# Softmax shifts and q laid in their rows by DMA instead of PE transposes and ScalarE copies, in an exact masked-attention layer

## The reference

```python
qkv = layer_norm(x, g1, be1) @ w_qkv            # (n, 3, 8, 16)
scores = einsum('nhd,mhd->hnm', q, k) * 16**-0.5
scores = where(adj != 0, scores, -inf)
out = einsum('hnm,mhd->nhd', softmax(scores, -1), v)
x = x + out @ w_proj + b_proj
x = x + gelu(layer_norm(x, g2, be2) @ w1 + b1) @ w2 + b2
```

## Time and profile before

| | |
|---|---|
| median of 3 runs | 1792.54 us (1791.68 to 1794.93) |
| profiled execution | 1792.59 us, span 1790.8 us |
| mean granted TensorE clock | 0.97 |
| first weighing of tile 4's step 3 to that of tile 5 | 204.25 us |

### The profile page before, as it was taken

How to read it: one execution, slowest core, us unless ns; L and a number is a source line. 1 busy time by engine, 2 the same in 40 slices (tenths; PEclk the granted TensorE clock), 3 DMA queues, 4 the chain that set the end, 5 groups by cost and what they waited for, 6 DMA issues and landing times.

```text
span 1790.8 us, 46610 instructions
## 1 busy us (share of the span) xinstructions
PE 1640.1 (92%) x17058; PEld 516.3 (29%) x17058; DVE 1411.1 (79%) x4471; ACT 1322.5 (74%) x1475; POOL 1198.3 (67%) x1129
## 2 busy tenths in 40 slices
PE   6989999999999999999999999999999999999975
PEld 3422222323223232323223232323223232223213
DVE  6888879877898779887898779988799778987501
ACT  4547877787877877787777878777777878778771
POOL 4945587578856777468856788558865788557441
PEclk9869999999999999999999999999999999999995
DMA  7710036202450035301360035301362024400000
GB/s 213 173 42 2 19 107 119 55 1 66 128 110 2 13 101 119 73 1 55 113 121 17 2 97 129 78 2 42 109 106 48 2 77 125 78 2 2 8 7 6
DMA packets 168711, 115.08 MB, mean 64 GB/s; under 512 B 139297, under 2 KB 149026, under 8 KB 168482
## 3 DMA queue, kind: packets, MB, share of 16 engines
q1 hardware_dynamic: 157730, 103.71, 24.2%
q10 hardware_dynamic: 10752, 8.39, 1.6%
HBM read 74.33 MB, written 4.19 MB: 44 GB/s over the span
## 4 chain that ended last, share of the span: by engine, by line
PE 61%; ACT 22%; issue 12%; DVE 2%; DMA 1%; POOL 1%; ACTq 0%; SPq 0%; DVEq 0%; POOLq 0%
ACT probs L738 19%; PE pv_ps L1034 17%; PE ring_ps L971 11%; PE score_ps L1123 11%; PE score_ps L1138 10%; PE score_ps L1057 2%; PE ring_ps L1091 2%; PE score_ps L1047 2%; ACT q_stack L623 2%; PE score_ps L995 2%; PE ring_ps L1082 1%; PE ring_ps L1067 1%; PE ring_ps L1074 1%; ACT halves L714 1%; DVE masked_out L773 1%
## 5 line engine op out<-in xcount | busy, mean ns | idle before, releaser
L773 DVE CUSTOM_DVE_ANT_0 masked_out<-ring_ps,row_mask 128x512 bf16<-128x512 f32 x2048 | 1310.6, 688 | 194.8 <-PE ring_ps L971 159.1
L738 ACT ACTIVATE probs<-score_ps,score_scale 128x1024 f32<-128x1024 f32 x1024 | 1088.0, 1112 | 355.0 <-PE score_ps L1138 346.8
L518 POOL TENSOR_TENSOR probs<-probs,keep 128x1024 int32<-128x1024 int32 x256 | 604.8, 2364 | 314.5 <-ACT probs L738 304.3
L1034 PE MATMUL pv_ps<-probs,v_ones 128*17 128x512 f32 x4096 | 542.4, 602 | 1.8 <-POOL probs L518 0.4
L971 PE MATMUL ring_ps<-k_stack,q_stack 51*64 51x512 f16 x4096 | 490.0, 398 | 13.6 <-DVE row_max L773 12.8
L1138 PE MATMUL score_ps<-q_stack,k_stack 51*64 51x512 f16 x4096 | 372.0, 391 | 32.2 <-ACT probs L738 13.0
L1123 PE MATMUL score_ps<-mask_t,ident_bf 64*64 64x512 bf16 x3072 | 274.8, 387 | 45.9 <-ACT probs L738 17.3
L971 PEld LDWEIGHTS ring_ps<-k_stack,q_stack 51*64 51x64 f16 x4096 | 166.5, 104 | 468.6 <-DVE row_max L773 403.9
L1138 PEld LDWEIGHTS score_ps<-q_stack,k_stack 51*64 51x64 f16 x4096 | 116.6, 104 | 243.5 <-PE score_ps L1123 181.8
L773 DVE DVE_READ_ACCUMULATOR2_ANT row_max<- 128x1 f32 x2048 | 169.7, 83 | 0.0
L1123 PEld LDWEIGHTS score_ps<-mask_t,ident_bf 64*64 64x64 bf16 x3072 | 93.4, 106 | 188.3 <-ACT probs L738 126.6
(11 more groups left out here) (117 smaller groups left out, 897.7 us busy)
## 6 DMA issues: line engine op xcount, KB each, us to landing
adj_in<-adj SPq DMA_DIRECT2D x128, 512.0 KB, 4.1
mask_t<-row_mask SPq DMA_TRANSPOSE x128, 3.8
xq<-xnT_dram ACTq DMA_DIRECT2D x8, 256.0 KB, 2.6
x_res<-x ACTq DMA_DIRECT2D x8, 256.0 KB, 4.1
out<-rows ACTq DMA_DIRECT2D x8, 256.0 KB, 4.6
xnT_dram<-attn ACTq DMA_DIRECT2D x4, 256.0 KB, 4.9
xnT_dram<-halves ACTq DMA_DIRECT2D x4, 256.0 KB, 2.5
w_sb<-L_gnn_w SPq DMA_DIRECT2D x2, 256.0 KB
```

The source lines that it names most:

```text
L518: nc.gpsimd.tensor_tensor(view, view, keep[:, KEPT.index(m), :].unsqueeze(1).broadcast_to([128, 2, TILE]), ALU.mult).then_inc(probs_masked, 1)
L738: nc.scalar.activation(probs[:, (2 * g + n) % SLOTS, :], score_ps[:, half:half + 2, :].rearrange("p a n -> p (a n)"), ACT.Exp, scale=score ...
L773: nc.vector.tensor_tensor_reduce(out=masked_out[:, place % 3, :], in0=ring_ps[:, place % 3, :], in1=row_mask[:, j, ch * 512:(ch + 1) * 512 ...
L1034: last = nc.tensor.matmul(pv_ps[32 * k:32 * k + HD + 1, :], v_ones[:, block_of(g, b), 2 * p + a, :], probs[:, (2 * g + b) % SLOTS, a * TIL ...
```

## The change

The shift fills go from the score ring. Where GpSimd has split a half's maxima, SP waits for it, writes `max_part` transposed to DRAM (1,024 elements of two bytes), waits for that to land, and loads it with two DMAs into the two shift rows of each half of `q_stack`; TensorE waits for these loads at the first scores of a quarter. The very first two shifts of the kernel stay as they were. q is made once a tile with the plain weights (`wq_all`) in a single fill at step 33; ScalarE takes a float16 part of it and the whole, GpSimd makes the low part (one subtraction, step 34), and SP stores both parts to DRAM and loads them with six DMAs into the stacked rows. TensorE waits for these at step 43. The two h2t fills become one at step 17; the four up fills move from steps 19 to 25 to steps 21 to 27, the down fills from 30 to 33 to 31 to 34, the store of the output by one step. SP's program now follows the steps: placements, then adjacency loads, then q, then mask transposes.

```diff
-UP_STEPS = [19 + 2 * f for f in range(FC)]
-ACT_FILLS = {16: ("h2t", 0), 17: ("h2t", 1), 31: ("q", 0), 35: ("q", 1), 37: ("q", 2), 41: ("q", 3)}
+UP_STEPS = [21 + 2 * f for f in range(FC)]
+ACT_FILLS = {17: ("h2t",), 33: ("q",)}
 ACT_FILLS.update({g: ("up", f) for f, g in enumerate(UP_STEPS)})
-for _p in range(1, PAIRS + 1):
-    ACT_FILLS.update({QUARTER * _p - 12: ("shift", _p % PAIRS, 0), QUARTER * _p - 2: ("shift", _p % PAIRS, 1)})
...
-DVE_FILLS.update({30 + s: ("down", s) for s in range(SUB)})
+DVE_FILLS.update({31 + s: ("down", s) for s in range(SUB)})
...
+def load_step(k):
+
+    return {n: g for g, n in zip(CONVERTS, range(CONVERTED))}[k - 2] if k >= 2 else 0
...
+        shift_dram = nc.dram_tensor("shift_dram", (2, 2 * 2 * SHIFT_PARTS, 128), F16, kind="Internal").ap()
+        q_dram = nc.dram_tensor("q_dram", (2, 2, DIM, TILE), F16, kind="Internal").ap()
...
+            def store_q(i, par):
+
+                sp.wait_ge(q_done, i + 1)
+                if i > 0:
+                    sp.wait_ge(q_in, i * (16 * 2 * len(PART_ROW)))
+                for low, part in enumerate((q_high, q_low)):
+                    sp.dma_start(q_dram[1 - par, low], part[:, :]).then_inc(q_stored, 16)
+
+            def load_q(i, par):
+
+                sp.wait_ge(q_stored, (i + 1) * 32)
+                settled(sp)
+                for n, first in enumerate(PART_ROW):
+                    heads = q_dram[1 - par, Q_LOW[n]].rearrange("(p a d) n -> a d p n", a=2, d=HD)
+                    for a in range(2):
+                        r = HALF * a + first
+                        sp.dma_start(q_stack[1 - par][r:r + HD, :, :], heads[a]).then_inc(q_in, 16)
+
+            def place_shift(i, par, p, jj):
+
+                n = neg_max_order(i + (p == 0), p, jj)
+                sp.wait_ge(split_step, SPLIT_OPS * (n + 1))
+                if n >= 4:
+                    sp.wait_ge(shift_in[jj], 32 * (n // 2 - 1))
+                with nc.allow_non_contiguous_dma(reason="maxima from partitions to a row"):
+                    sp.dma_start(shift_dram[jj].rearrange("c q -> q c"),
+                                 max_part[:, jj, :, :].rearrange("q c k -> q (c k)")).then_inc(shift_out, 16)
+                sp.wait_ge(shift_out, 16 * (n - 1))
+                settled(sp)
+                for a in range(2):
+                    r = HALF * a + SHIFT_ROW
+                    sp.dma_start(q_stack[par if p else 1 - par][r:r + SHIFT_PARTS, p, 256 * jj:256 * (jj + 1)]
+                                 .rearrange("k (j q) -> k j q", j=2),
+                                 shift_dram[jj].rearrange("(j a k) q -> a k j q", a=2, k=SHIFT_PARTS)[a])\
+                      .then_inc(shift_in[jj], 16)
...
+                for g in range(STEPS):
+                    if c and g in SPLITS and (b or SPLITS[g][0] > 0):
+                        place_shift(i, par, *SPLITS[g])
+                    for k in range(CONVERTED):
+                        if b and g == load_step(k):
+                            sp.wait_ge(flag_done, (i + 1) * CONVERTED + (k - 5))
+                            load_adj((i + 1) * SUB + k // ADJ_C, k % ADJ_C, k % 2)
+                    if b and g == Q_STEP + 1:
+                        store_q(i, par)
+                    if b and g == Q_STEP + 2:
+                        load_q(i, par)
+                    for f in range(ADJ_C):
+                        if b and g == chunk_step(f):
+                            chunk_masks(i, f, (b, c, d))
...
+                    if b and g == Q_STEP:
                         pool.wait_ge(score_taken, made(SCORES, i, bcd, ACT_PLACE[g - 1]))
                         settled(pool)
-                        nc.gpsimd.tensor_tensor(q_stack[1 - par][:, Q_ADDS[g], :], q_x[:, :], q_neg[:, :], ALU.add)\
-                          .then_inc(q_done, 1)
+                        nc.gpsimd.tensor_tensor(q_low[:, :], q_x[:, :], q_high[:, :], ALU.subtract).then_inc(q_done, 1)
...
-                    nc.scalar.activation(q_neg[:, :], bank, ACT.Identity, scale=part_coef[:, 0:1])
+                    nc.scalar.copy(q_high[:, :], bank)
                     nc.scalar.copy(q_x[:, :], bank).then_inc(score_taken, 1)
-                elif what[0] == "shift":
-                    store_shift(q_stack[par if what[1] else 1 - par], bank, what[1], what[2]).then_inc(score_taken, 1)
...
+                nc.vector.tensor_scalar(wq_all[:, :], wqkv[:, 0:DIM], grow[:, 0:1], None, ALU.mult).then_inc(w_rep, 1)
+
+            for a in range(2):
+                nc.vector.memset(q_stack[1][HALF * a + SHIFT_ROW:HALF * (a + 1), :, :], 0.0).then_inc(q_clear, 1)
...
+                    pe.wait_ge(xq_loaded, (i + 1) * 16)
+                    last = nc.tensor.matmul(bank, wq_all[:, :], xq[:, :], start=True, stop=True)
...
+                    if ahead == 1 and (g, x) == (STEPS - AHEAD, 0):
+                        pe.wait_ge(q_in, (i + 1) * (16 * 2 * len(PART_ROW)))
...
+                    if g % QUARTER == 0 and n == 0 and (i > 0 or p > 0):
+                        for jj in range(2):
+                            pe.wait_ge(shift_in[jj], 32 * (neg_max_order(i, p, jj) // 2))
```

More of the change, by code:

```diff
@@ L89, with chunk_step @@
 POOL_LN2 = [12, 13, 14, 15, 16, 18]
-STORE_STEP = 34
+STORE_STEP = 35
 XQ_STEP = 44
 SEEN_STEP = 50
+def load_step(k):
+    return {n: g for g, n in zip(CONVERTS, range(CONVERTED))}[k - 2] if k >= 2 else 0
+def chunk_step(f):
+    return STEPS - QUARTER + (f + 1) * PER_C // BLOCKS - 1
 def made_for(what):
-    if what[0] == "q" or what[:2] == ("shift", 0):
+    if what[0] == "q":
         return "b"
-    if what[0] == "shift" or (what[0] in ("sums", "back") and what[1] < FOURS - 1):
+    if what[0] in ("sums", "back") and what[1] < FOURS - 1:
         return "c"
@@ L257, in program @@
         ident_h = sb("ident_h", [128, 128], F16)
-        wq_rep = sb("wq_rep", [DIM, PAIRS, 128], F32)
+        wq_all = sb("wq_all", [DIM, DIM], F32)
         w1_sb = sb("w1_sb", [DIM, DIM_FF], F32)
@@ L640, in _ @@
             root(0)
+            act.wait_ge(q_clear, 2)
             act.wait_ge(w_in, 16 * 5)
@@ L1044, in act_fill @@
                 if what[0] == "q":
[L1045 to L1050 removed]
+                    pe.wait_ge(xq_loaded, (i + 1) * 16)
+                    last = nc.tensor.matmul(bank, wq_all[:, :], xq[:, :], start=True, stop=True)
                 elif what[0] == "h2t":
[L1052 to L1054 removed]
+                    pe.wait_ge(ln2_applied, (i - 1) * (SUB + 1) + SUB)
+                    for s in range(SUB):
+                        last = nc.tensor.transpose(bank[:, 128 * s:128 * (s + 1)], rows2[:, s, :], ident[:, :])
                 elif what[0] == "up":
```

56 lines of the change are left out of this document (20 added, 36 removed).

## The result

The changed kernel takes 2216.14 us (median of 4 runs, 2207.18 to 2223.26) where the kernel before takes 1792.11 (4 runs beside it): a ratio of 1.236, 95% interval 1.231 to 1.241. Forecast were 1730 us and faster. The profiled execution took 2207.18, its span is 2205.0.

The account below looks back on a forecast made before the run. TensorE and VectorE together were taken as the floor, in a loop every extra piece of work lengthens. Gains of 60.9 in seven tiles and 2.9 in the last, less 1.2 outside, gave 1792.6 - 62.6 = 1730 us, range 1712 to 1760.

Parts of the forecast that it names:

- The step that failed: SP's placements: the write of 1,024 two-byte maxima to DRAM lands in 4 us, priced near the small DMA rows.
- the prediction's own sign of being wrong: Wrong if the write takes over 6 us, TensorE's weighing waits for GpSimd in steps 46 to 56, or freed steps miss 2.80.
- The bounds around it, 3.6 and 7: Write of maxima: 3.6 us from small loads of 128 and 512 elements, 7 allowed above a 256 KB store's 4.9.
- The reverse: SP's round trip bounds the loop: past 6 us of write, about 2 a tile per microsecond; 1817 at 12; chance 0.06.
- Cost: 0: Placements on SP and DMA engines: GpSimd waits about a microsecond at step 46, covered by its maskings' room; cost 0.
- the first rival: Slow placements hold GpSimd up at steps 38, 46: 7 us write costs 2.4 a tile, 1747; 0.24 shared with GpSimd floor.
- the sum itself: Seven tiles at 8.7 us give 60.9, last tile 2.9, less 1.2 outside the loop: 62.6 us gained.
- step 4 (shift beside sums): Step 4, shift fill beside a VectorE fill (sums), 3.77 us: removing the shift gives 0.15, between nothing and 0.76.
- The 0.5 of GpSimd stall: Steps 18 to 27: masking delayed behind a split takes back 0.5 of the 1.58 us gain, leaving 1.1.
- the second rival: Shifts beside sums come off whole and clock dips vanish: up to 9.6 and 6 us more, 1714 to 1724; chance 0.16.
- more comes off: Case that the time falls to 1712 to 1722 us, below the forecast as told; chance 0.16.
- stores and loads of q are hidden: q path from step 35: stores 4.9, six issues, loads 4.1, 11 us, with some 21 before step 43 reads: hidden.

Follow-up runs that it names:

- The writes alone: Kernel before plus 62 packed element writes of a constant that nobody waits for, SP ordered by steps as in the change, shifts still by fills: 2195.31 us.
- the cheap version: Whole change, but maxima written to DRAM as 128 rows of 16 bytes and loaded as contiguous rows, values permuted (timing only): 1719.87 us, ratio 0.958 against the kernel before.
- 1815.99: Whole change, but each half's maxima leave in four writes of 32 partitions and return in four loads: 1815.99 us, ratio 1.012 against the kernel before.
- the later order: Whole change with four writes and four loads, but SP loads shift rows two steps after their writes, q in two portions: 1739.33 us, ratio 0.970 against before.

## Why the prediction was wrong

**The step that failed** is the one on the write: "I take 4, near the small rows, since these share the form." It measured 14.6, and so the prediction's own sign of being wrong, a write over 6 us, is what came. The bounds around it, 3.6 and 7, were wrong too. The lower priced by elements, from rows in which contiguous DRAM bytes are *read* into SBUF, the upper by a store of 256 KB in long rows; what cost was that 128 partitions write into the same 256 bytes. No row before shows a DMA that does that, so the honest upper bound was wider than 7; and the cheap spacing of 32 bytes shows that it wasn't the "scattered" in "scattered small writes" that I had to allow for, but the opposite.

**The reverse had its mechanism half.** The slower rival ("SP's round trip becomes the loop's bound") puts break-even a little past 10 us and 1817 at 12. Carried on to 14.6 by its own rule, 2 us a tile for each past 6, it gives 17.2 a tile, 120 in seven, about 1850. Its places are right: 149.2 us of TensorE's waits for shift rows, 91.1 of GpSimd's for adjacency loads. But 366 us are missing above that, and most of them are the second mechanism, which no rival had: while such a DMA is in flight for 14 us, engines stop that don't wait for it. The writes alone show its size, 403 us. The two overlap, so they don't add up to the whole exactly: from the cheap version's 1719.87 to 2216.14 it is 496 us, 403 by that run and 93 left for late rows and loads.

**"Cost: 0" of what is added on SP** held with the cheap DMAs (1.7 us a wait), and no longer at 7.0 us a write, where the first rival had 2.4 a tile. There it was (1815.99 - 1739.33) / 7 = 11 us a tile, if all that the later order gave back is put down to it. The first rival counted a longer write alone. In that run SP also issues four loads a placement and not two (2.5 us), and the six q loads stand in the same queue (2.7 to 4.0 us).

**The clock.** I left it as it was (0.97). After, it is 0.876: over step 63 of tile 3, where TensorE is idle for 15 of 18.47 us, the granted clock is 0.64 on the mean, and PE's busy sum rises from 1640.1 to 1728.8 for fewer instructions. Stalls cost more than their length.

**What held** was the sum itself, seen where nothing stalls, in the kernel with the cheap DMAs (tile 4):

| stretch | before | forecast gain | measured gain |
|---|---|---|---|
| steps 14, 46 | 3.56 | 0.76 each | 0.76, 0.77 |
| step 62 | 3.55 | 0.76 | 0.53 (mean of inner tiles 0.73) |
| step 52 | 3.68 | 0.88 | 0.75 |
| step 4 (shift beside sums) | 3.77 | 0.15 | 0.11 |
| step 36 (shift, sums, q) | 5.05 | 1.40 | 1.39 |
| step 40 (q) | 3.95 | 1.15 | 1.20 |
| steps 18 to 27 | 34.05 | 1.1 | 1.60 |
| steps 30 to 35 | 24.19 | 1.73 | 2.54 |

The 0.5 of GpSimd stall that I took off in steps 18 to 27 didn't come. In steps 30 to 35 the pair 34 to 35 came to 6.4 where I had 7.26. And the second rival was right that the clock dips go: before, three of six inner tiles have 25.6 to 25.7 us there, and with the cheap DMAs none has more than 22.0. A tile is 195.5 us on the mean, where I had 196. So the forecast for the work removed, 62.6, was 74 when measured with cheap DMAs, and the case "more comes off" would have been the right one had the write cost nothing. Also right: stores and loads of q are hidden. The chance that I gave to "slower", 0.06, was too small by more than bad luck: it rested on the table's medians, none of which is of a write like this one.

## What to carry to other kernels

Before a DMA that lays many partitions' elements side by side in DRAM is put in a loop, measure that one form by itself, in flight beside the real work: a price from other small DMAs says nothing about it. Space such elements by 32 bytes or more, or split the write so that few of them share a row; and ask of every slow DMA not only who waits for it but whose completions come late beside it. Where a view can't name what ended a wait, look in the kernel for what the wait is for, and count the suspect's packets in stretches with and without a stop before you believe in it. Where a queue must wait for a round trip, issue, do other things, and come back: the same DMAs in another order were 77 us apart.

## What the runs showed of the hardware that I had not expected

- 128 two-byte elements from 128 partitions into one 256-byte row of DRAM land in 16.8 us, 1,024 into eight rows in 14.2 to 15.0; at 8 bytes apart in 4.0, from 32 bytes on in 2.1 to 2.8.
- While such a write is in flight, completions of other DMAs wait for it, on SP's queue (copy within SBUF 12.9 to 14.3 us, alone 1.2) and on ScalarE's (13.6 to 14.0, beside a spaced write 2.3 to 2.8), though the copy's packets are recorded within 2 us.
- TensorE stops in such flights for up to 11.5 us without waiting for any of the kernel's DMAs, and VectorE and ScalarE with it: 62 writes that nobody waits for cost 403 us; spaced by 512 bytes, nothing. All of these waits (244 in five kernels) are for semaphores that TensorE's own matmuls raise, dated 1.5 to 11.4 us after the matmuls; GpSimd's increments come through.
- A gather of 512 two-byte elements of DRAM onto two partitions takes 6.4 us; a read of 1,024 contiguous ones across 128 partitions 2.4.
